# Latent attention with its scores made twice: queries on partitions for the maximum, keys on partitions for the probabilities

## The reference, cut to what matters

```python
latent_kv = (x @ Wk + x @ Wv) @ W_down_kv
k_rec, v_rec = latent_kv @ W_up_k, latent_kv @ W_up_v
scores = einsum('bhqd,bhkd->bhqk', heads(x @ Wq), heads(k_rec)) * scale      # scale = 1/16
scores = clip(scores, -1e4, 1e4)
decay = exp(-1e-4 * abs(idx[:, None] - idx[None, :]))
attn = softmax(clip(scores * decay, -1e4, 1e4), axis=-1)
out = einsum('bhqk,bhkd->bhqd', attn, heads(v_rec)) @ Wo
```

## Time and profile before

| what | value |
|---|---|
| median of 3 runs | 1646.94 us |
| profiled execution, its own time | 1639.76 us |
| its span, first to last instruction | 1638.2 us |
| PE, DVE, ACT, POOL busy | 1362.9, 920.3, 930.2, 190.5 us |
| latent_projections and before | 0 to 83.4 us |
| latent_attention, first stack DMA to last attn_sb write | 83.4 to 607.2 us |
| mean granted TensorE clock | 0.886 |

### The profile page before, as it was taken

How to read it: one execution, slowest core, us unless ns; L and a number is a source line. 1 busy time by engine, 2 the same in 40 slices (tenths; PEclk the granted TensorE clock), 3 DMA queues, 4 the chain that set the end, 5 groups by cost and what they waited for, 6 DMA issues and landing times. The chain is left out here.

```text
span 1638.2 us, 36440 instructions
## 1 busy us (share of the span) xinstructions
PE 1362.9 (83%) x12288; PEld 968.8 (59%) x12291; DVE 920.3 (56%) x2059; ACT 930.2 (57%) x1793; POOL 190.5 (12%) x546
## 2 busy tenths in 40 slices
PE   5779999999999976898265699888984479999992
PEld 3357777777777755444223463363454269999992
DVE  5568888888888855432789754562344223233233
ACT  3479999999999972345375477524431023333330
POOL 0011111111111110111100000021120611111110
PEclk8879999999999998869656899997796589999996
DMA  3411101011010132100000100041006211111115
GB/s 124 133 40 26 28 20 29 20 28 25 23 28 20 29 100 64 51 1 4 16 1 0 31 2 1 4 176 66 1 4 209 92 38 39 35 35 38 36 32 164
DMA packets 60026, 74.30 MB, mean 45 GB/s; under 512 B 13007, under 2 KB 47729, under 8 KB 59953
## 3 DMA queue, kind: packets, MB, share of 16 engines
q1 hardware_dynamic: 53168, 56.76, 11.6%
q0 software_dynamic: 4672, 14.50, 2.7%
q10 hardware_dynamic: 2112, 2.10, 0.4%
HBM read 50.43 MB, written 22.88 MB: 45 GB/s over the span
## 5 line engine op out<-in xcount | busy, mean ns | idle before, releaser
L659 DVE CUSTOM_DVE_ANT_0 probs_sb<-banks,decay_sb 128x1024 f32<-128x1024 f32 x256 | 308.1, 1221 | 43.5 <-PE banks L578 22.4
L706 ACT ACTIVATE probs_sb<-probs_sb,shift_sb 128x1024 f32<-128x1024 f32 x256 | 294.8, 1151 | 18.1 <-POOL shift_sb L563 16.4
L588 PEld LDWEIGHTS banks<-ident_sb,probs_sb 128*128 128x128 f32 x2048 | 238.4, 141 | 55.0 <-issue 23.2
L588 PE MATMUL banks<-ident_sb,probs_sb 128*128 128x128 f32 x2048 | 267.9, 274 | 0.8 <-ACT probs_t_sb L521 0.8
L521 ACT ACTIVATE probs_t_sb<-banks 128x512 f32<-128x512 f32 x384 | 214.6, 597 | 4.1 <-PE banks L588 2.3
L578 PE MATMUL banks<-k_stack_sb,q_stack_sb 96*128 96x512 bf16 x512 | 157.1, 390 | 13.9 <-DMA k_stack_sb<-k_parts 10.7
L603 PE MATMUL banks<-probs_t_sb,v_head_sb 128*32 128x128 f32 x4096 | 151.2, 277 | 0.7 <-ACT probs_t_sb L521 0.7
L1836 PEld LDWEIGHTS banks<-slots_xt_sb,tile_w_sb 128*128 128x128 f32 x1248 | 146.8, 194 | 1.9
L1836 PE MATMUL banks<-slots_xt_sb,tile_w_sb 128*128 128x128 f32 x1248 | 147.0, 277 | 0.0
L1848 PE MATMUL banks<-experts_w_sb,xt_sb 128*128 x624 | 141.2, 380 | 1.5 <-issue 1.5
L1882 ACT ACTIVATE slots_xt_sb<-banks 128x256 f32<-128x256 f32 x39 | 14.9, 383 | 214.1 <-PE banks L1822 214.1
(11 more groups left out here) (289 smaller groups left out, 1948.0 us busy)
## 6 DMA issues: line engine op xcount, KB each, us to landing
experts_w_sb<-in_L_ffn_W SPq DMA_DIRECT2D x16, 1024.0 KB, 12.0
q_stack_sb<-q_parts SPq DMA_DIRECT2D x192, 32.0 KB, 1.7
k_stack_sb<-k_parts SPq DMA_DIRECT2D x192, 32.0 KB, 1.8
slots_x<-zeros_sb POOLq DMA_DIRECT2D x1, 5031.0 KB, 22.8
slots_x_sb<-slots_x SPq DMA_DIRECT2D x39, 129.0 KB, 2.1
xt_sb<-outputs_y SPq DMA_DIRECT2D x8, 512.0 KB, 5.7
q_parts<-parts_sb SPq DMA_DIRECT2D x8, 384.0 KB, 3.0
k_parts<-parts_sb SPq DMA_DIRECT2D x8, 384.0 KB, 4.2
```

The source lines that it names most:

```text
L588: last = pe.transpose(k.ps[:, 4 + half, j * P:(j + 1) * P], pr[:, s % 4, (half * TPG + j) * P:(half * TPG + j + 1) * P], k.ident[:, :])
L659: dve.tensor_tensor_reduce(out=pr[:, s % 4, :], in0=scores, in1=decay[:, off:off + S], scale=1.0, scalar=-3.0e38, op0=ALU.mult, op1=ALU.ma ...
L706: act.activation(pr[:, s % 4, :], pr[:, s % 4, :], ACT.Exp, bias=shift[:, s % 8:s % 8 + 1], accum_out=sums[:, (s // TPG) % 4, s % 4:s % 4 ...
```

## The change

latent_projections makes each query and key tile in two versions, multiplied along the token axis by exp(-1e-4 t) and exp(+1e-4 t) (new constant `fade`, two rows broadcast to all partitions). A product of a query of one version and a key of the other has the decay in it on one side of the diagonal; the two pairings serve the two sides. So 32 pieces are faded, split and stored instead of 16; the third part moves from DVE to POOL. The scratch tensors double.

latent_attention works in 16 groups of 4 heads x 512 queries of one batch. Each score is made twice: in tiles of 128 queries x 1024 keys for the maximum (DVE multiplies by `inner`, which mends the diagonal block, and throws the product away), and in units of 128 keys x 512 queries of one head, with three more rows in the stacks that hold minus the maximum in three bf16 parts, so that ACT's exponential of the PSUM bank is at once the transposed probability. The diagonal blocks are made a second time for the other side of the diagonal (one more unit for each diagonal key tile), and POOL zeroes the wrong triangles with affine_select. Row sums come from a column of ones in the values. All loops over groups are unrolled.

The maxima of a group go POOL (split in three), PE (turn), ACT (copy), SP (6 DMAs into the query stacks), and PE's key-side scores of the group wait for them (`peaks_in`). SP issues all of the stack loads, in this order: those of groups 1 and 2, the maxima of group 0, then for each group its maxima and the loads of the group two ahead. The loads of group 0 stand in latent_projections between its stores. The units use a ring of three PSUM banks.

The diff, cut (the clipping path, the value staging and the declarations are left out):

```diff
 def latent_projections(k, v_heads, fade, stacks):
+            def apply_fade(e):
+                n, version = divmod(e, 2)
+                dve.wait_ge(qk_ready, n + 1)
+                wait(dve, part3_done, e - 3)
+                side = version if is_query(e) else 1 - version
+                half = n // 4 % 2
+                dve.scalar_tensor_tensor(out=rest[:, e % 4, :], in0=k.ps[:, n % 4, :], scalar=scale if is_query(e) else 1.0,
+                                         in1=fade[:, side, half * G:(half + 1) * G],
+                                         op0=ALU.mult, op1=ALU.mult).then_inc(faded, 1)
+
+            def subtract_first(e):
+                dve.wait_ge(part1_done, e + 1)
+                dve.tensor_tensor(rest[:, e % 4, :], rest[:, e % 4, :], parts[:, e % 4, 0, :],
+                                  ALU.subtract).then_inc(rest1_done, 1)
+                if bounds(e):
+                    own.did(dve.tensor_reduce(largest[:, e // 2:e // 2 + 1], parts[:, e % 4, 0, :], AX, ALU.max,
+                                              apply_absolute_value=True))
+
+            for e in range(NV + 1):
+                if e < NV:
+                    apply_fade(e)
+                if e > 0:
+                    subtract_first(e - 1)
...
+        @block.gpsimd
+        def _(pool):
+            for e in range(NV):
+                pool.wait_ge(part2_done, e + 1)
+                pool.wait_ge(rest1_done, e + 1)
+                pool.tensor_tensor(parts[:, e % 4, 2, :], rest[:, e % 4, :], parts[:, e % 4, 1, :],
+                                   ALU.subtract).then_inc(part3_done, 1)
...
+                if e == 20:
+                    for x in range(4):
+                        sp.wait_ge(stored[x], 16 * 4)
+                if e >= 20 and (e - 20) % 3 == 0:
+                    load_stacks(sp, stacks, 0, (e - 20) // 3)
+            for x in range(4):
+                sp.wait_ge(stored[x], 16 * (NV // 4))
...
+def load_stacks(eng, stacks, g, h):
+
+    n, half = divmod(g, 2)
+    b, first = divmod(n * HEADS, H)
+    rows = slice(b * D + (first + h) * HD, b * D + (first + h + 1) * HD)
+    for version in range(2):
+        row = 0
+        for r in range(3):
+            copies = 3 - r
+            for x in range(copies):
+                dst = slice(row + x * HD, row + (x + 1) * HD)
+                if half == 0:
+                    eng.dma_start(stacks.k[dst, n % 2, version, h, :],
+                                  stacks.k_scratch[version, x, rows, :]).then_inc(stacks.arrived[0][h], 16)
+                eng.dma_start(stacks.q[dst, g % 3, version, h, :],
+                              stacks.q_scratch[version, r, rows, half * G:(half + 1) * G]).then_inc(stacks.arrived[half][h], 16)
+            row += copies * HD
...
 def latent_attention(k, v_heads, attn, decay, inner, stacks):
...
+            def store_peaks(g):
+                sp.wait_ge(peaks_copied, g + 1)
+                for version in range(2):
+                    for r in range(PARTS):
+                        sp.dma_start(stacks.q[ROWS + r:ROWS + r + 1, g % 3, version, :, :].rearrange("p h n -> p (h n)"),
+                                     peak_rows[r * TILES:(r + 1) * TILES, g % 2, :]).then_inc(peaks_in, 16)
+
+            for g in range(1, 3):
+                for h in range(HEADS):
+                    load_stacks(sp, stacks, g, h)
+            store_peaks(0)
+            for g in range(1, GROUPS):
+                store_peaks(g)
+                if g + 2 < GROUPS:
+                    sp.wait_ge(key_scored, g * UNITS)
+                    for h in range(HEADS):
+                        load_stacks(sp, stacks, g + 2, h)
...
+            def key_scores(g, i, h):
+
+                item = (exp_done, unit_index(g, i, h) + 1)
+                if i == 0 and h == 0:
+                    pe.wait_ge(peaks_in, (g + 1) * 2 * PARTS * 16)
+                wait_for_bank(pe, item)
+                edge = min(max(block_of(g, i) * P, 0), G)
+                if edge > 0:
+                    last = key_product(g, i, h, bank_of(item), 1, 0, edge, 0)
+                if edge < G:
+                    last = key_product(g, i, h, bank_of(item), 0, edge, G, edge)
+                last.then_inc(key_scored, 1)
...
+            def sum_values(s):
+
+                g, i = divmod(s, QT)
+                n, kt = g // 2, key_tile(g, i)
+                pe.wait_ge(exp_done, unit_index(g, i, HEADS if on_diagonal(i) else HEADS - 1) + 1)
+                if i == 0:
+                    pe.wait_ge(v_staged, n + 1)
+                    wait(pe, mix_copied, g)
+                if on_diagonal(i):
+                    pe.wait_ge(selected, s // 2 + 1)
+                    lo = block_of(g, i) * P
+                    for h in range(HEADS):
+                        pe.matmul(k.ps[VW * h:VW * (h + 1), PV_BANK, lo:lo + P], vh[:, n % 2, h, kt, :],
+                                  probs_d[:, s // 2 % 2, h, :], start=False, stop=False, skip_group_check=True)
+                for h in range(HEADS):
+                    last = pe.matmul(k.ps[VW * h:VW * (h + 1), PV_BANK, :], vh[:, n % 2, h, kt, :], probs_of(s)[:, h, :],
+                                     start=i == 0, stop=i == QT - 1, skip_group_check=True)
+                last.then_inc(summed, 1)
...
+            pe.wait_ge(constants, 2)
+            for tile in range(TILES + LEAD):
+                scores(tile)
+                if tile == TILES + 1:
+                    turn_peaks(0)
+            for g in range(GROUPS):
+                for i in range(QT):
+                    if g * QT + i >= 2:
+                        sum_values(g * QT + i - 2)
+                    for x in range(2):
+                        for h in range(2 * x, 2 * x + 2):
+                            key_scores(g, i, h)
+                        if x == 1 and i == 6 and g + 1 < GROUPS:
+                            turn_peaks(g + 1)
+                        if tile_at(g, i, x) < GROUPS * TILES:
+                            scores(tile_at(g, i, x))
+                    if on_diagonal(i):
+                        diagonal_scores(g, i)
+                    if i == 3 and g > 0:
+                        turn_mix(g - 1)
+            for s in range(GROUPS * QT - 2, GROUPS * QT):
+                sum_values(s)
+            turn_mix(GROUPS - 1)
...
+            def select(g, i):
+                s = g * QT + i
+                lo = block_of(g, i) * P
+                later = probs_of(s)[:, :, lo:lo + P]
+                pool.wait_ge(exp_done, unit_index(g, i, HEADS - 1) + 1)
+                pool.affine_select(later, later, [[0, HEADS], [1, P]], ALU.is_ge, 0.0, base=0, channel_multiplier=-1)
+                earlier = probs_d[:, s // 2 % 2, :, :]
+                pool.wait_ge(exp_done, unit_index(g, i, HEADS) + 1)
+                pool.affine_select(earlier, earlier, [[0, HEADS], [-1, P]], ALU.is_gt, 0.0, base=0,
+                                   channel_multiplier=1).then_inc(selected, 1)
...
+            def highest(tile):
+                g, x = divmod(tile, TILES)
+                dve.wait_ge(scored, tile + 1)
+                wait(dve, peaks_split, g - 1)
+                wait(dve, peaked, tile - 1)
                 dve.nop(nofuse=True)
+                dve.tensor_tensor_reduce(out=junk[:, tile % 2, :], in0=tile_scores(tile), in1=inner[:, window(tile)],
...
...
+            def exponential(g, i, h):
+                u, s = unit_index(g, i, h), g * QT + i
+                act.wait_ge(key_scored, u + 1)
+                act.wait_ge(released, u + 1)
+                if h == 0:
+                    wait(act, summed, s - 2)
+                if h < HEADS:
+                    out = probs_of(s)[:, h, :]
+                else:
+                    wait(act, summed, s - 3)
+                    out = probs_d[:, s // 2 % 2, :, :].rearrange("p h n -> p (h n)")
+                act.activation(out, k.ps[:, bank_of((exp_done, u + 1)), :], ACT.Exp).then_inc(exp_done, 1)
```

More of the change, by code:

```diff
@@ L299, in project_out, with latent_projections @@
         k.stats_known = True
-def latent_projections(k, v_heads, q_scratch, k_scratch):
+def latent_projections(k, v_heads, fade, stacks):
     nc = k.nc
@@ L438, in _ @@
         def _(sp):
-            for n in range(NP):
+            for e in range(NV):
+                n, version = divmod(e, 2)
                 g, s = divmod(n, 4)
@@ L442, in _ @@
                 m = s % 2
[L443 to L451 removed]
+                scratch = stacks.q_scratch if s < 2 else stacks.k_scratch
@@ L457, in latent_attention, with stacks_arrived @@
+def stacks_arrived(eng, stacks, g, h):
+    n, half = divmod(g, 2)
+    eng.wait_ge(stacks.arrived[half][h], (n + 1) * 16 * (24 if half == 0 else 12))
+def latent_attention(k, v_heads, attn, decay, inner, stacks):
     nc = k.nc
     k.next_block()
-    stack_in = [k.sem(f"stack_in{u}") for u in range(2)]
-    scored, clipped, peaked, shifted = (
-        k.sem("scored"), k.sem("clipped"), k.sem("peaked"), k.sem("shifted"))
```

(38 more changed lines are left out.)

520 lines of the change are left out of this document (270 added, 250 removed).

## The result

The changed kernel takes **1835.76 us** (median of 4 runs, 1834.60 to 1838.44), the kernel before on the same chip 1644.06 (4 runs). The ratio is **1.1186, with 95% between 1.1138 and 1.1234**; it leaves out one of the four runs of the kernel before, at 1670.07 us, which was in a slower state of the chip. The profiled execution has a span of 1832.8 us, 194.6 more than before.

What follows compares the result with a forecast made beforehand. The prediction took ACT to bound the kernel before and SP's DMA issue the changed one. Adding 53.9 (latent_projections), 110.6 (latent_attention) and 4 (the end), +168.5, to the profiled 1639.8 gave 1808 us, range 1715 to 1880.

Steps and rivals of the forecast that it cites:

- SP's issue as the bound: In latent_attention, 1152 DMAs issued in order on SP's one queue at 0.458 us each, 528 us of issue.
- The head, 70.5 us: From the stage's first DMA to group 0's key side: 144 loads 66.0, maxima 2.75, landing 1.75 us.
- Nine short steps, 260.9: Start to start of groups with a short load list behind them, 29.5 us each, two without the clock's loss.
- Six long steps, 280.5: Groups 2, 4 to 12 with 96 loads behind them: 44.0 plus 2.75 for the maxima, 46.75 us each.
- Group 15, 22.5: The last group, without query-side tiles: starts at 611.9 and takes 22.5 us, so the stage ends at 634.4.
- latent_projections, +53.9: Time to the next stage's start, 137.3 for 83.4 us: 2.08 us a piece to piece 20, then SP's issue binds.
- the ring of four buffers: In latent_projections, four part buffers may bind more than DVE's 1.7 us: 8.3 us for four, 2.08 a piece.
- The engines alone, 442 us for the stage: latent_attention if only engines counted: lead 30, 15 steps of 26, last group 22.5 us; 82 less than before.
- the cheap rival: DMA issue is cheap enough, below a break-even of 0.27 us, so engines bind: 1578 us, 7 in 100.
- The clock after a wait: PE restarts at a low clock after long waits: 4.5 us at half rate, 2.3 lost, 25 us for 23.
- the rival with a clock that stays low: PE stays at 1.2 GHz after each wait, seven groups up to 23 us more each: 1953 us, 8 in 100.
- The end, +4: POOL's store of zeros now comes after the last select, some 4 us closer to the stage's end: +4 us.

Runs made afterwards that it cites:

- e2: The changed kernel with every stack load from group 4 on moving only 64 columns, same number of DMAs: 1844.48 us, ratio 1.1292 to the kernel before.
- e3: The changed kernel with one DMA loading both versions of a stack part, 24 or 48 a group: 1647.92 us, ratio 1.0078 to the kernel before.
- e12: The kernel before with each stack load cut in two halves of the columns, 768 loads for 384: 1643.33 us, ratio 1.0045.
- e10: e6 with the store of zeros at the start of group 14 and the next queries made before the values: 1583.98 us, ratio 0.9656.
- e6: e3 with minus-one rows written in latent_projections, group 0's maxima before group 2's loads, two maxima DMAs for six: 1604.44 us, ratio 0.9818.
- e1: The changed kernel with one DMA for all four heads of each version and part, 12 or 24 a group: 1657.7 us, ratio 1.0141.
- e7: e6 with POOL's store of zeros issued in group 8 instead of behind the last group: 1600.25 us, ratio 0.9799.
- e8: The kernel before with POOL's store of zeros issued ahead of its loop: 1633.42 us, ratio 0.9987.
- e11: e10 with group 0's stacks loaded by 24 DMAs of four heads instead of 48 of one: 1588.84 us, ratio 0.9682.

## Why the prediction was right, and where it was off

- **SP's issue as the bound, 0.458 us each: right.** The loads start 0.46 us apart at 16 KB and at 32. By e2 bytes don't matter, by e3 halving the number removes every long step, by e12 384 extra issues cost 4.6 us where ACT is the bound. The rivals with a cheap issue fall. The 50 ns of the Trainium skill ("DMA: Bandwidth & Descriptors", "Anatomy of one DMA — SWDGE (gpsimd) path") are a sequencer's dispatch on the path of GpSimd. The prediction tried them as a price on SP's queue, where the pitch is nine times that.
- **The head, 70.5 us**: 71.8 (key side from 215.28), by the mechanism forecast: the maxima go out at 210.3, when the 144 loads are through. In part this was luck. The lead had no term for POOL's constants, and PE's first scores waited for them until 160.94, 17.4 us after the first load; SP's list was long enough to hide it.
- **Nine short steps, 260.9**: 257.6, between 27.0 and 30.3.
- **Six long steps, 280.5: mis-sized by 19.2**, mean 49.95 us for 46.75. The maxima DMAs, costed at 0.458 from loads, take 0.61 each (3.67 for six; they are 4.0 KB, not the 8 of the prediction), 0.9 us a step. The 96 loads take 45.9 to 46.7 for 44.0, because now and then one takes longer (363.24: 1.49 us).
- **Group 15, 22.5**: 27.8. Without query-side tiles PE hardly gets faster: it waits 2.6 us in nine pieces for banks that exponentials hold, and 1.7 at the end for a select and the copy of the mix. What makes up the rest of the 5.3 isn't shown. Timeline rows of it:

```profile
778.57 0.82 PE L646 MATMUL banks<-q_stack_sb,k_stack_sb 99*128 99x512 bf16 x3
779.65 0.39 PE L646 MATMUL banks<-q_stack_sb,k_stack_sb 99*128 99x512 bf16 x1 [0.26 <-ACT probs_sb L907]
```

- **The stage, +110.6**: +133.0. The four differences (1.3 - 3.3 + 19.2 + 5.3, with roundings 22.4) are the whole miss in the stage.
- **latent_projections, +53.9: +60.1, with the wrong mechanism.** A piece takes 2.29 us for 2.08 (eight in 18.35 us). I blamed the ring of four buffers; the rows of 41 to 86 us say DVE:

```profile
L431 POOL TENSOR_TENSOR parts_sb<-rest_sb,parts_sb 128x512 bf16<-128x512 f32 x21 | 28.9, 1390 | 55.3 <-ACT parts_sb L447 54.9
L398 DVE TENSOR_TENSOR rest_sb<-rest_sb,parts_sb 128x512 f32<-128x512 f32 x21 | 20.0, 953 | 0.0
L392 DVE SCALAR_TENSOR_TENSOR rest_sb<-banks,fade_sb 128x512 f32<-128x512 f32 x21 | 14.3, 680 | 8.5 <-PE banks L358 8.5
...
L401 DVE TENSOR_REDUCE largest_sb<-parts_sb 128x1 f32<-128x512 bf16 x10 | 6.7, 673 | 0.0
```

  The subtraction, costed at 686 ns, takes 953 on the average: with 680 and half of 673 that is 1.97 us a piece, for 1.7. The average hides two kinds (timeline of the changed kernel, 46.5 to 50 us; the second instruction of the merged row starts at 46.87):

```profile
45.25 2.77 POOL L431 TENSOR_TENSOR parts_sb<-rest_sb,parts_sb 128x512 bf16<-128x512 f32 x2
...
47.01 1.56 DVE L398 TENSOR_TENSOR rest_sb<-rest_sb,parts_sb 128x512 f32<-128x512 f32 x1
...
49.09 0.68 DVE L398 TENSOR_TENSOR rest_sb<-rest_sb,parts_sb 128x512 f32<-128x512 f32 x1
...
49.31 1.47 POOL L431 TENSOR_TENSOR parts_sb<-rest_sb,parts_sb 128x512 bf16<-128x512 f32 x1 [1.29 <-ACT parts_sb L447]
```

  Of 22 subtractions from 39 to 86.5 us, 14 take the 0.67 to 0.68 us that were costed. Six take 1.56 or 1.57, and each of these starts 0.13 to 0.14 us after one of POOL's; the two that start late in one of POOL's take 0.78 and 1.05. So the third part, moved to POOL, still cost DVE time, and the prediction put that at nothing. No run takes POOL's work away; the trace alone shows it. ACT did wait 6.8 us in this stretch for stores of earlier pieces to land, which is the ring, but no wait of DVE hangs on it. DVE's only idle time, 8.5 us, is for PE at the turns between groups, where the values stand before the next queries; e10, which puts the queries first, starts the loads 5.8 us earlier. The rest is the tail: 58.2 us from group 0's first stack load (85.29) to the stage's first load, for 55.7.
- **The engines alone, 442 us for the stage: too low for this kernel.** In e3, with SP off the path, it takes 490.0: the lead 45.9 for 30, fifteen steps of 27.6 for 26, the last group 29.5 for 22.5. The 446.6 of e6 come near 442 only without the constants in the lead and with two DMAs for six. The "+16" of latent_projections with free loads also holds only with 1.7 us a piece; with the 2.08 of the sum it is about +28. So the cheap rival's 1578 us was too low: e3's profiled execution, with 48 issues left in latent_projections, spans 1641.7. In the parts, exponentials were taken at 0.555 and follow each other 0.48 to 0.50 apart (records of 0.60 that overlap); selects of 0.3 to 1.5 us take 0.635 and hold PE 1.0 us at one place:

```profile
L907 ACT ACTIVATE xt_sb<-banks 128x512 f32<-128x512 f32 x344 | 179.4, 603 | 213.0 <-PE banks L646 213.0
...
L764 POOL TENSOR_SCALAR_AFFINE_SELECT xt_sb<-xt_sb 128x512 f32<-128x512 f32 x43 | 27.3, 635 | 359.3 <-ACT xt_sb L907 359.3
```

- **The clock after a wait: 2.3 us were taken.** The windows above show 0.90 in the 30 us after a long wait and 1.00 in the 28 after that, so an estimated 3 us at most. The six short steps of groups 3 to 13, behind long waits, take 28.5 to 30.3 us, those of groups 1 and 14 27.6 and 27.0, so 2 us more on the average; group 0's, 27.25, doesn't show it. It came back every time; the rival with a clock that stays low is out.
- **The end, +4**: +5. The rest of the program was taken as unchanged, and was 3.6 us shorter.

## What to carry to other kernels

Count the DMAs of every queue and multiply by the pitch at which the trace shows them issued back to back: where the product nears the time of the stage, the queue is the bound, however small the transfers, and below that it costs nothing but at the head of the stage. A short DMA on which the next step waits doesn't belong behind a prefetch list; have it cover several rows at once, and merge prefetches only until the queue is off the path, as larger ones land later. Work moved to another engine can still cost the first one time: look at single durations beside the other engine's, not at the mean. Judge a change of one stage by that stage's length as well as by the total, because the clock elsewhere can give some of it back.

## What the runs showed of the hardware

- Three partitions don't make a memset cheap: 16384 bf16 elements on each of 3 took POOL 13.75 us (0.84 ns an element of one partition). Unseen behind SP's loads in the changed kernel, it came onto the path once SP was off it.
- A VectorE subtraction of 128x512 whose two operands lie in SBUF takes 0.68 us, and 1.56 when it starts 0.13 to 0.14 us behind a like subtraction of POOL; started first, it takes 0.68 and POOL's takes 1.47 to 1.67 instead of 1.15 (latent_projections, above).
- Issue time follows the shape: 0.46 us for a load of 16 or 32 KB, 0.47 with 64 or 128 KB (e1), 0.61 for 16 partitions of 256 bytes going into one row (on ACT's queue too, 3.72 for six), and 0.74 where one DMA takes 48 partitions into three rows (1.48 for two in e6), less than half of what the three it replaces cost.
- A store of 5 MB that spreads over all DMA engines held up DMAs of 12 KB issued 1.7 us behind it on another queue by about 10 us (e7, once).
- The granted clock of a later stage, cross_attention, lay at 0.84 to 0.92 in some of these kernels (before, changed, e3, e6, e7) and at 0.50 to 0.69 in others (e8 to e11) that differ only in work long done, in one profiled execution of each. From PE's return to the end they take 1011.0 to 1016.4 us and 1017.0 to 1026.4.
